# A fused attention and expert block on one core: three buffers of projection rows, constants moved between VectorE's first steps, modulation products ahead of the first keys, and a separate signal for the second half of the first group's keys

## What is computed

```python
mod = (silu(c) @ wmod).reshape(4, 6, 1, 256)      # sa, ca, ga, sb, cb, gb
h = layernorm(x) * (1 + ca) + sa
q, k, v = keep_top(h @ wq.T), keep_top(h @ wk.T), keep_top(h @ wv.T)   # 16 heads of 16 features,
                                                   # keep_top leaves the largest |feature| per head
scores = q @ k.T / 4, causal; the 64 largest per query stay, then softmax
x = x + ga * (attn @ v) @ wo.T
h = layernorm(x) * (1 + cb) + sb
gates = softmax(h @ router_w + router_b)           # each of 8 experts takes its 512 best tokens
x = x + gb * sum over experts of gate * (relu(h @ w1 + b1) @ w2 + b2)
```

## Time and profile before

| | us |
|---|---|
| median of 3 runs | 1011.04 (1010.74 to 1011.15) |
| the profiled execution, its own time | 1013.74 |
| its span in the trace | 1012.0 |
| first product of scores starts | 64.62 |
| the expert part starts | about 705 |

### The profile page before, as it was taken

How to read it: one execution, slowest core, us unless ns; L and a number is a source line. 1 busy time by engine, 2 the same in 40 slices (tenths; PEclk the granted TensorE clock), 3 DMA queues, 4 the chain that set the end, 5 groups by cost and what they waited for, 6 DMA issues and landing times. The chain is left out here.

```text
span 1012.0 us, 16390 instructions
## 1 busy us (share of the span) xinstructions
PE 844.4 (83%) x6080; PEld 461.5 (46%) x6080; DVE 657.9 (65%) x1504; ACT 454.5 (45%) x572; POOL 320.2 (32%) x466
## 2 busy tenths in 40 slices
PE   6766989989989979989978978883018999999996
PEld 5532444434444434434434534342014777666664
DVE  6848597678687786696794795544876644544441
ACT  2426566765557756466666567641002111222210
POOL 3612433421533512244432212100005443343222
PEclk9859999999999999999999999996557999999998
DMA  4000000000200002200002102002902443442111
GB/s 146 22 1 1 22 2 20 2 1 2 63 15 8 1 15 72 64 1 1 2 1 86 42 1 86 1 22 77 383 3 65 116 105 61 119 115 32 22 21 21
DMA packets 34851, 46.51 MB, mean 46 GB/s; under 512 B 2184, under 2 KB 30928, under 8 KB 34640
## 3 DMA queue, kind: packets, MB, share of 16 engines
q1 hardware_dynamic: 28624, 36.89, 10.9%
q0 software_dynamic: 6144, 8.52, 5.1%
HBM read 32.69 MB, written 12.72 MB: 45 GB/s over the span
## 5 line engine op out<-in xcount | busy, mean ns | idle before, releaser
L937 ACT ACTIVATE p_buf<-ps 128x1024 f32<-128x1024 f32 x288 | 279.4, 1023 | 173.6 <-PE ps L410 154.8
L776 POOL TENSOR_SCALAR_AFFINE_SELECT p_buf<-p_buf 128x512 f32<-128x512 f32 x128 | 98.3, 792 | 325.1 <-ACT p_buf L937 237.6
L410 PE MATMUL ps<-qx,kd 32*128 32x512 f32 (+3 forms) x1280 | 134.0, 511 | 32.4 <-DVE p_buf L1273 12.9
L438 PE MATMUL ps<-p_buf,vv 128*17 128x512 f32 (+3 forms) x1664 | 152.7, 468 | 4.9 <-DVE p_buf L1273 2.7
L2105 ACT ACTIVATE h_t<-ps,b_t 128x512 f32<-128x512 f32 x64 | 44.0, 687 | 237.5 <-PE ps L2045 237.5
L1273 DVE SCALAR_TENSOR_TENSOR p_buf<-ps,p_buf 128x1024 f32<-128x1024 f32 x64 | 78.3, 1223 | 87.3 <-PE ps L432 46.0
L2055 PE MATMUL ps<-w_sb,h_t 128*128 128x256 f32 x512 | 112.5, 380 | 0.8 <-ACT h_t L2105 0.8
L2045 PE MATMUL ps<-tok_t,w_sb 128*128 128x512 f32 x256 | 113.1, 600 | 0.0
L2055 PEld LDWEIGHTS ps<-w_sb,h_t 128*128 128x128 f32 x512 | 96.6, 190 | 15.3 <-ACT h_t L2105 1.6
L410 PEld LDWEIGHTS ps<-qx,kd 32*128 32x128 f32 x1280 | 56.7, 188 | 98.7 <-issue 94.3
L354 PE MATMUL ps<-w_t,h_t 128*128 128x512 f32 (+1 forms) x224 | 78.5, 494 | 9.0 <-DVE p_buf L1273 5.2
(11 more groups left out here) (288 smaller groups left out, 1247.9 us busy)
## 6 DMA issues: line engine op xcount, KB each, us to landing
w_sb<-in_L_ffn_w_dram SPq DMA_DIRECT2D x16, 1024.0 KB, 8.4
h_table<-xr SPq DMA_DIRECT2D x3, 1056.0 KB, 4.6
x_in<-in_L_attn_x_dram SPq DMA_DIRECT2D x6, 512.0 KB, 4.0
out_dram<-xr SPq DMA_DIRECT2D x3, 1024.0 KB, 5.2
xr<-in_L_attn_x_dram SPq DMA_DIRECT2D x3, 1024.0 KB, 5.7
h_table<-xr SPq DMA_DIRECT2D x2, 528.0 KB, 3.4
xr<-in_L_attn_x_dram SPq DMA_DIRECT2D x2, 512.0 KB, 5.3
p_buf<-in_L_wmod_dram SPq DMA_DIRECT2D x1, 1024.0 KB, 8.5
```

What stands on the lines that cost most here:

```text
L410: m = pe.matmul(o, key, qx[r, par, t0:t0 + w], start=True, stop=not run)
L438: m = pe.matmul(ps[32 * h:32 * h + HD + 1, 6, o:o + w], vv[:, (gi // NG) % 2, i, HG * (gi % NG) + h, :], p_of(gi, u)[:, h, lo:lo + w], sta ...
L776: m = pool.affine_select(p, p, [[0, HG], [1, P]], ALU.is_ge, 0.0, base=0, channel_multiplier=-1)
L937: act.activation(p_of(gi, u)[:, 2 * a:2 * a + 2, :], buf(w), ACT.Exp, scale=0.25).then_inc(free_of(w)[0], 1)
```

## The change

- `y_abs`, `y_val` and `y_one` get three buffers; every wait on `f_keep` goes back three tiles instead of two, in group 0 and in the later batches.
- `constants` is cut in four (`one_per_head`, `clear_out_bank`, `pair_constants`, `sign_constants`), each called between VectorE's first steps, ahead of the first tile's `one_feature`.
- PE calls `other_mod` and then, behind K0, `mod_as_rows` ahead of Q0; K1 goes ahead of `own_key`; Q1 goes behind the scores of unit 0, and the scores of unit 1 of group 0 go ahead of `lost`.
- ScalarE lays out keys and queries apart, takes the modulation's columns ahead of K0 and its rows behind Q0.
- VectorE's work on the first keys is cut anew. Of the second half only the maximum is taken ahead of the signal `f_kp`, which then covers the first half's keys. The second half follows and signals `f_late`, for which the scores of unit 2 wait. The second half's scan and query mask (`second_half_queries`) move into the loop, behind the first two masks. PE waits for `f_uq` in front of `chosen` for the second half of group 0, not in front of the first scores.
- GpSimd's 60 fills move behind the last group.

The diff, cut to its core:

```diff
-        y_abs = sf("y_abs", [P, 2, 3 * NH, HD])
+        y_abs = sf("y_abs", [P, 3, 3 * NH, HD])
...
                     if u == 0:
                         pe.wait_ge(f_kp, gi + 2)
-                        pe.wait_ge(f_uq, gi + 2)
+                        if gi:
+                            pe.wait_ge(f_uq, gi + 2)
                     if gi == 0 and u == 2:
-                        mod_as_rows()
+                        pe.wait_ge(f_late, 1)
...
                     if a == 0 and c == 0:
                         pe.wait_ge(f_wk, gi + 1)
                         m_drained(("W", gi))
+                    if gi == 0 and c == 1 and a == 0:
+                        pe.wait_ge(f_uq, 2)
...
-                for k in range(15):
-                    for m in range(3):
-                        pool.memset(bit_u[:, k, m:m + 1], (m + 1) << (28 - 2 * k))
-                    pool.memset(bit_f[:, k:k + 1], float(1 << (28 - 2 * k)))
                 for gi in range(GA):
...
+                for k in range(15):
+                    for m in range(3):
+                        pool.memset(bit_u[:, k, m:m + 1], (m + 1) << (28 - 2 * k))
+                    pool.memset(bit_f[:, k:k + 1], float(1 << (28 - 2 * k)))
                 pool.wait_ge(s_const, 2)
...
-                stage_half(0)
+                stage_half("K", 0)
                 evict_y(0, 7)
                 act.wait_ge(f_ones, 1)
+                take_mod_cols()
                 rows("K0", 0)
+                stage_half("Q", 0)
                 rows("Q0", 0)
-                take_mod_cols()
-                stage_half(1)
+                take_mod_rows()
+                stage_half("K", 1)
+                stage_half("Q", 1)
                 rows("K1", 0)
-                rows("Q1", 0)
...
                     exps(gi, 0)
+                    if gi == 0:
+                        rows("Q1", 0)
                     exps(gi, 1)
-                    if gi == 0:
-                        take_mod_rows()
...
+                def first_rank():
+                    dve.tensor_tensor(k_max1[:, :], k_max1[:, :], mx[:, RUN - 1:RUN], ALU.max)
+                    m_full(("G", 0))
+                    dve.tensor_scalar(z_rank[:, :], ps[:, 7, 0:P], 15872.0, 2.0 ** -6, ALU.add, ALU.max).then_inc(f_mfree, 1)
+                    dve.tensor_scalar(k_far[:, 0:512], k_not[:, 0:512], -FAR, None, ALU.mult)
...
+                def first_keys_ready():
+                    dve.wait_ge(f_mfree, m_at["K1", 0] + 1)
+                    h = slice(0, 512)
+                    dve.tensor_reduce(k_max[:, :], kd[:, 0, 512:T], AX.X, ALU.max)
+                    dve.drain()
+                    dve.tensor_tensor(k_max[:, :], k_max[:, :], k_max1[:, :], ALU.max)
+                    dve.drain()
+                    dve.tensor_scalar(ks[:, 0, :], ks[:, 0, :], k_max[:, :], None, ALU.subtract)
+                    dve.wait_ge(f_mfree, m_at["Q0", 0] + 1)
+                    dve.scalar_tensor_tensor(qm[:, 0, :], mx[:, :], k_max[:, :], qx[:, 0, 0:RUN], ALU.subtract, ALU.mult)
+                    dve.scalar_tensor_tensor(kd[:, 0, h], kd[:, 0, h], k_max[:, :], k_far[:, h], ALU.subtract, ALU.add)
                     dve.drain().then_inc(f_kp, 1)
...
                 silu()
                 norm_stats(0, 0)
                 take_c()
+                one_per_head()
                 normalize(0, 0)
+                clear_out_bank()
                 take_first_mod()
+                pair_constants()
                 modulate(0, 0)
                 norm_stats(0, 1)
+                sign_constants()
                 normalize(0, 1)
                 one_feature(0, 0)
                 modulate(0, 1)
-                one_feature(0, 1)
-                constants()
-                for t in range(2, NT):
+                for t in range(1, NT):
                     one_feature(0, t)
                 first_half_keys()
+                first_rank()
+                first_keys_ready()
+                losers(0)
                 first_half_queries()
-                zero_rank(0)
-                losers(0)
+                first_weights()
                 second_half_keys()
-                second_half_queries()
...
                     mask(gi, 0, 1)
                     if gi == 0:
+                        second_half_queries()
                         router_constants()
```

More of the change, by code:

```diff
@@ L558, in _ @@
                     project(0, t)
+                other_mod()
                 rows("K0", 0)
+                mod_as_rows()
                 rows("Q0", 0)
-                other_mod()
                 pe.wait_ge(f_ones, 1)
                 zero_rank(0)
+                rows("K1", 0)
                 own_key(0)
-                rows("K1", 0)
-                rows("Q1", 0)
                 for gi in range(GA):
@@ L574, in _ @@
                     scores(gi, 0)
+                    if gi == 0:
+                        rows("Q1", 0)
+                        scores(gi, 1)
                     lost(gi)
@@ L581, in _ @@
                         weights_o(b)
-                    scores(gi, 1)
+                    if gi:
+                        scores(gi, 1)
                     chosen(gi, 0, 0)
@@ L902, in take_mod_rows, with stage_half @@
                     act.drain().then_inc(f_mraw, 1)
-                def stage_half(half):
+                def stage_half(kind, half):
                     act.wait_ge(f_keep, 4 * half + 4)
                     ts = slice(4 * half, 4 * half + 4)
-                    for dst, lo in ((k_st, NH), (q_st, 0)):
-                        for s in range(2):
-                            m = act.activation(dst[:, 0, ts, :, s, :], qk[:, ts, lo:lo + HG, :], ACT.Copy)
-                        m.then_inc(f_stage, 1)
+                    dst, lo = (k_st, NH) if kind == "K" else (q_st, 0)
+                    act.activation(dst[:, 0, ts, :, 0, :], qk[:, ts, lo:lo + HG, :], ACT.Copy)
+                    act.activation(dst[:, 0, ts, :, 1, :], qk[:, ts, lo:lo + HG, :], ACT.Copy).then_inc(f_stage, 1)
                 def evict_y(b, t):
@@ L1044, in m_full, with one_per_head @@
                     dve.wait_ge(f_mfull, m_at[k] + 1)
[L1046 to L1047 removed]
+                def one_per_head():
                     dve.memset(onesz[:, :, :], 0.0)
@@ L1129, in first_half_queries, with first_weights, second_half_queries @@
                     dve.drain().then_inc(f_uq, 1)
+                def first_weights():
+                    with nc.allow_low_precision("compared with half-integers of seven bits"):
+                        dve.reciprocal(wk_r[:, :], z_rank[:, :]).then_inc(f_wk, 1)
                 def second_half_keys():
-                    dve.wait_ge(f_mfree, m_at["K1", 0] + 1)
                     h = slice(512, T)
                     dve.tensor_scalar(k_not[:, h], kd[:, 0, h], 0.0, None, ALU.is_le)
+                    dve.drain()
+                    dve.tensor_scalar(k_far[:, h], k_not[:, h], -FAR, None, ALU.mult)
+                    dve.drain()
+                    dve.scalar_tensor_tensor(kd[:, 0, h], kd[:, 0, h], k_max[:, :], k_far[:, h], ALU.subtract,
+                                             ALU.add).then_inc(f_late, 1)
+                def second_half_queries():
+                    h = slice(512, T)
                     dve.tensor_copy(carry[:, :], left[:, 511:512])
```

44 lines of the change are left out of this document (18 added, 26 removed).

## The result

The changed kernel takes **1000.98 us** (median of 4 runs, 997.98 to 1005.54) against 1011.1 for the kernel before (median of 4 runs beside it, 1010.74 to 1013.76): a ratio of 0.9891, with a 95% interval of 0.9865 to 0.9917. The forecast was 999.5, with 996 to 1005 as its range.

A forecast was written before the change was run, and what follows sets the result against it. Order bounds the kernel until the second mask, VectorE behind it. That mask 16.1 us earlier less 2.5 given back is 13.6, or 9.3 if the clock falls; 11.5 taken: 1011.04 - 11.5 = 999.5 us, range 996 to 1005.

The forecast's parts named there:

- `mod_as_rows`: Modulation rows on PE ahead of Q0: 2.6 us at full clock, against 3.93 before, mostly at half clock.
- given back: `second_half_queries` moved behind the masks, where VectorE is the limit, costs 2.5 to 3.2 us there.
- The clock: PE's clock falls to half around 50 us, in short pieces with gaps; second mask at 65.7, gain 9.3 us.
- The first rival: Clock falls already in `other_mod`, `mod_as_rows` takes 5.2 us, K1's keys at 53.8; 1002.6 to 1005.1 us; chance 0.19.
- the full-clock end of the forecast: Second mask at 61.4 instead of 77.52 with PE at full clock: 16.1 us earlier, 13.6 after 2.5 given back.
- the forecast's 4.3 us: Cost of a clock fall around 50 us on the way to the second mask: 65.7 instead of 61.4.
- K0: K0's keys out at 44.1 instead of 44.76, only 0.6 us gained, because the modulation stands in front.
- mod_as_rows at the second mask: Of the second mask's 16.1 us, the last four come from `mod_as_rows` no longer standing ahead of it.
- Free edits: Constants in VectorE's gaps and GpSimd's moved fills cost 0; third buffers alone end the last tile at 41.9, not 45.3.
- with two buffers this does not heal: In the projection stretch, the tiles' chain with two buffers leaves the last tiles about 3 us behind PE.
- Slower through the clock in the loop: Rival: shifted waits in the group loop lower the clock, 2.7 us an episode, six giving 1015.7; chance 0.03.

The follow-up runs named there:

- again: The changed kernel unaltered, timed more often and traced once more: 999.69 us, ratio 0.9875, span 1000.3.
- after: The changed kernel's first profiled execution, slowest of its four runs: 1005.54 us, span 1003.8.
- mr_back: Changed kernel with `mod_as_rows` back in front of the scores of unit 2, and ScalarE's copy of the rows behind the second exponentials: 1002.85 us, ratio 0.9909.
- queries_first: Changed kernel with `second_half_queries` (second half's scan and query mask) ahead of the group loop again: 999.48 us, ratio 0.9869.
- two_buf: Changed kernel with `y_abs`, `y_val` and `y_one` in two buffers again, waits set back: 1000.5 us, ratio 0.9887.
- k0first: Changed kernel with K0 turned ahead of `other_mod`, and Q0 ahead of `mod_as_rows`, ScalarE's copies in the same order: 999.2 us, ratio 0.9879.
- consts_back: Changed kernel with VectorE's thirteen constants in one piece between the second and third tile's `one_feature`, three buffers kept: 1000.3 us, ratio 0.9888.
- trim_qf: Changed kernel with `other_mod` cut to the one block that is read and `second_half_queries` ahead of the loop again: 994.96 us, ratio 0.9832.
- fill2: Changed kernel with 7 unread products of 256 columns between the blocks of `other_mod`, in a free bank, no wait added: 1001.98 us, ratio 0.9899.
- trim: Changed kernel with `other_mod` cut to the one block that is read, 8 instead of 32 small products, and one VectorE addition dropped: 997.5 us, ratio 0.9861.
- trim_k0: Changed kernel with `other_mod` cut to the one block that is read and K0 turned ahead of it: 996.0 us, ratio 0.9851.
- fill: Changed kernel with 11 unread products of 256 columns, four inside `other_mod`, seven in PE's gaps behind it: 1006.93 us, ratio 0.9936.

## Why the prediction was right, point by point

The time (999.5 forecast, 1000.98 and 999.69 measured) was right, and so was the ground of it: the gain is made ahead of the second mask, and VectorE bounds what comes behind. That it came so near is in part luck, since the clock did not do what was forecast. Its steps:

| | before | forecast | again | after |
|---|---|---|---|---|
| K0's keys out | 44.76 | 44.1 | 43.92 | 44.72 |
| `mod_as_rows` | 3.93 | 2.6 | 4.44 | 5.25 |
| K1's keys out | 58.51 | 50.2 | 51.69 | 53.56 |
| first scores | 64.62 | 52.8 | 54.36 | 56.28 |
| second mask | 77.52 | 61.4 to 65.7 | 62.45 | 66.37 |
| given back | | 2.5 to 3.2 | 2.66 | 2.65 |

By these rows the 15.07 us of again are 6.82 from K1's keys being out earlier, 3.44 from the shorter way from them to the first scores (2.67 us instead of 6.11), and 4.81 from the way on to the second mask (8.09 instead of 12.90). Only of the last was a part undone in a run, by mr_back. No run puts K1 behind `own_key` again, Q1 ahead of the scores, or all of the second half's keys ahead of `f_kp`: how the first two parts divide among these moves and the clock is read from the traces and argued, not shown.

- **The clock was the step that failed.** "I expect it to fall here too, around 50" put the fall behind `mod_as_rows`. It fell at 42 to 43 in both traces, inside `other_mod` or half a us behind its end; so `mod_as_rows` was mis-sized, 4.44 and 5.25 instead of 2.6 (2.74 at full clock, so the size itself was right). That is 1.8 us in again, and K1's keys and the first scores are late by 1.5 and 1.6 for it. The first rival, with a chance of 0.19, had named this and the row that spoke for it (four-column products that did not lift the clock). Its chance was too small: what counted against it, twenty dense microseconds just before, did not hold the clock, in these two or in the six other traces that have the 32 products unbroken. A fall around 50 to 52 did come as well in three of the eight (the first trace, queries_first, two_buf), as a second one, and in mr_back the clock stayed low from 42.4 to about 59.
- **What made the time come out nonetheless.** In again the fall at 43 was over at 46.5, and none followed around 50: the second mask is 1.05 from the full-clock end of the forecast. In after a second one followed at 52, and the execution took 1005.54. It cost less than the forecast's 4.3 us: the clock was back at about 62, ahead of the scores of unit 2, and from the first scores to the second mask were 10.1 us against 8.1 in again. The rival's sums fit that execution: K1's keys at 53.8 (measured 53.56), a gain of 8.4 (the spans give 8.2). The forecast of 11.5 between 13.6 and 9.3 fits again: 15.07 - 2.66 = 12.4 there, 11.7 by the spans. The median of the runs lies between the two. So the middle of the range was met in part by luck: an early fall, which was not in the sum, came in place of the late one, or ahead of one shorter than assumed.
- **K0.** "This step gives only 0.6, because the modulation stands in front of it" was right, 0.0 and 0.8. k0first shows that the remedy would have given nothing.
- **mod_as_rows at the second mask.** "The last four come from `mod_as_rows` no longer standing there": mr_back puts it back, the mask waits 3.43 us, and the two masks are 2.65 us further apart; the kernel takes 3.2 more, part of it by the clock.
- **Given back.** 2.65, the scan 1.70 with GpSimd beside it, between the bounds of 1.28 and 2.01.
- **Free edits.** Right: the constants and the fills change nothing that the runs can tell. Nor do the third buffers, 0.8 us at most, for which the prediction had given the last tile's end (42.0 measured, 41.9 forecast) and no price of their own. But it gave that end to "the third buffers alone", and this was wrong: with three buffers and the constants in one piece the last mark ends at 44.52 (consts_back), with two buffers and the constants spread at 42.79 (two_buf), before at 45.31. Most of the 3.3 us is the constants' doing, and "with two buffers this does not heal" does not hold once they are moved. What hides all this from the time is PE's 8 us of modulation products.
- **Slower through the clock in the loop.** It did not come to that: 914.3 and 914.7 us behind the fourth mask, against 914.0.

Not settled: why the clock comes back at 46.5 in one execution and only at about 49, to fall again at 52, in the other; what moves the part behind the fourth mask by 4.6 us between traces; and whether trim_qf's 994.96 owes anything to its queries, since the intervals of the three trimmed kernels overlap.

## What to carry to other kernels

Where several small pieces go through one engine ahead of the first real work, ask of each what it blocks and who reads it: a move worth up to 3 us stood beside 24 products that nobody read, and cutting these took another 2 to 3 us off the medians. Price a matrix engine's piece at both clocks, and look in a trace at what the clock did over pieces like it before you count on the higher one. Before you advance a piece, look for what else its reader waits for: the first keys 2.6 us earlier gave nothing while the modulation rows and the last tile's mark stood behind them.

## What the runs showed of the hardware

- In all eight traces in which the 32 products of four columns stand unbroken behind the projections, the clock fell from 2.4 to 1.2 GHz at 41.9 to 43.2 us, with PE busy all the time since 28.6. With 7 products of 256 columns between them it stayed up to 52.2 (fill2). With 8 small ones it stayed up to 45.7 where the 512-column products followed (trim), and fell at 42.7 where PE first waited 1.91 us (trim_k0). In fill, behind a wait of 1.69 us, it fell at 43.5 while products of 256 columns ran.
- VectorE's running scan over 512 elements takes 1.23 us alone and 1.95 beside GpSimd's `keep`; a tile's mark (128x768) takes 0.96 us where it starts just ahead of a product of `keep` (38.30 and 38.31 us in again), which then takes 1.48 instead of 0.67, and 1.78 where it starts just behind one (42.74 and 42.55 in consts_back). The Trainium skill, "GPSIMD Engine Reference", section on specifications, says that the two share their way into the memory when VectorE reads two inputs; the scan reads two tiles, and the trace agrees.
- One program, nine runs: 997.98 to 1005.54 us, and the kernel before 1008.6 to 1015.6 us in 16. The way to the second mask differed by 3.9 us between two traces of the same program: a single trace of such a kernel can mislead by as much.
